# Four chained layers in one kernel: seams between stages joined, a mixing product cut into pieces and run among attention scores, and a top-4 choice made with an eight-largest instruction

## What is computed

```python
for l in range(4):
    xn = layernorm(x)
    x = x + attn[l](xn) * silu(ffn[l](xn))
```

```python
# layer 0 attn: gated linear recurrence; its last step adds a bias
out = h_m @ W_out + b_out
# layer 0 ffn: shared expert + 8 experts, two chosen by the router's logits = x @ router_w
# layer 1 attn: selective scan; starts with W_in, W_skip, a convolution over 4 taps
# layer 1 ffn: dense 1024-wide; layer 2 attn: 16 heads of 16, one key head
# layer 2 ffn: 16 experts, four chosen, at most 128 tokens an expert, and a shared expert
scores = softmax(x @ gate_w.T); topk_w, topk_i = top_k(scores, 4)
y = scatter_add(expert outputs); return y + shared
# layer 3 attn: 16 heads, keys and values from a latent of 64 numbers a token
probs = softmax(q @ kv.T * scale); out = (probs @ kv) @ W_o
# layer 3 ffn: weights in four bits
inter = gelu(x @ Wg.T) * (x @ Wu.T); out = inter @ Wd.T
```

## Time and profile before

| what | us |
|---|---|
| median of 3 runs | 1033.92 (1033.4 to 1038.56) |
| profiled execution, its own time | 1034.3 |
| its span | 1032.5 |
| PE busy | 948.9 (92%) |
| DVE busy | 696.2 (67%) |
| ACT busy | 480.4 (47%) |
| POOL busy | 279.5 (27%) |

### The profile page before, as it was taken

One profiled execution on the slowest core, in us unless ns is written; L12 is line 12 of the kernel. 1 busy time (PEld: TensorE's weight loads), 2 busy tenths in 40 slices (PEclk: granted clock), 3 DMA queues, 4 the chain that ended last, 5 costly groups with the idle time before them and its releaser, 6 DMA issues. The chain is left out here.

```text
span 1032.5 us, 13682 instructions
## 1 busy us (share of the span) xinstructions
PE 948.9 (92%) x4708; PEld 568.6 (55%) x4708; DVE 696.2 (67%) x1092; ACT 480.4 (47%) x1008; POOL 279.5 (27%) x244
## 2 busy tenths in 40 slices
PE   4999998999999999999999999887889859999997
PEld 2555564365665666655555555565466535555554
DVE  2789867369998999759545555674775735566653
ACT  3542224799887887322135555535664611111112
POOL 0000000008887888420014233102643520000000
PEclk9899999999999999999999999999999989999999
DMA  4112205040000000028045443221000001111101
GB/s 130 43 66 77 71 11 178 1 119 26 22 22 21 22 21 1 2 85 250 1 131 112 91 111 84 56 62 41 2 1 2 1 1 31 61 31 30 30 1 41
DMA packets 58303, 53.89 MB, mean 52 GB/s; under 512 B 14216, under 2 KB 53224, under 8 KB 58240
## 3 DMA queue, kind: packets, MB, share of 16 engines
q1 hardware_dynamic: 52704, 47.05, 15.2%
q0 software_dynamic: 3072, 4.20, 2.5%
q10 hardware_dynamic: 2464, 1.84, 0.6%
HBM read 44.45 MB, written 5.47 MB: 48 GB/s over the span
## 5 line engine op out<-in xcount | busy, mean ns | idle before, releaser
L1085 POOL TENSOR_TENSOR seen<-state,c_row 128x512 f32<-128x512 f32 x128 | 160.7, 1278 | 101.4 <-DVE state L1105 74.2
L1105 DVE TENSOR_TENSOR_SCAN state<-decay,banks 128x512 f32<-128x512 f32 x128 | 155.3, 1217 | 14.8 <-issue 7.3
L2526 PE MATMUL banks<-xnT,weight 128*128 128x512 f32 x256 | 115.0, 592 | 1.1 <-PEq L2221 1.1
L1043 ACT ACTIVATE weighed_x<-dx_tok,b_tok 128x512 f32<-128x512 f32 x124 | 87.6, 709 | 25.7 <-PE banks L1215 24.4
L2237 POOL TENSOR_TENSOR prob<-prob,inverse 128x512 f32<-128x512 f32 x64 | 65.3, 1041 | 116.4 <-DVE inverse L2324 116.4
L1053 ACT ACTIVATE decay<-delta_pairs,A 128x510 f32<-128x510 f32 x128 | 90.5, 707 | 6.2 <-DVE state L1105 6.2
L1215 PEld LDWEIGHTS banks<-ident,weighed_x 128*128 128x128 f32 x512 | 58.6, 140 | 59.2 <-ACT weighed_x L1043 33.3
L2558 ACT ACTIVATE gelu<-banks 128x512 f32<-128x512 f32 x32 | 19.1, 597 | 138.1 <-PE banks L2526 138.1
L1215 PE MATMUL banks<-ident,weighed_x 128*128 128x128 f32 x512 | 80.1, 279 | 2.3 <-DVE state L1105 2.3
L2526 PEld LDWEIGHTS banks<-xnT,weight 128*128 128x128 f32 x256 | 48.6, 190 | 49.4 <-issue 47.9
L1229 PE MATMUL banks<-seen,fold 128*64 128x512 f32 x256 | 69.7, 617 | 0.0
(11 more groups left out here) (382 smaller groups left out, 1717.0 us busy)
## 6 DMA issues: line engine op xcount, KB each, us to landing
prob_row<-probs_dram SPq DMA_DIRECT2D x8, 512.0 KB, 3.7
c_row<-c_dram SPq DMA_DIRECT2D x32, 128.0 KB, 2.8
slot_wide_w<-in_L_ffn_w_gate SPq DMA_DIRECT2D x16, 176.0 KB, 2.4
slot_wide_w<-in_L_ffn_w_up SPq DMA_DIRECT2D x16, 176.0 KB, 2.5
slot_down_w<-in_L_ffn_w_down SPq DMA_DIRECT2D x16, 176.0 KB
gate_up_w<-in_L_ffn_gate_up_w SPq DMA_DIRECT2D x8, 256.0 KB, 2.7
delta_pairs<-conv_in SPq DMA_DIRECT2D x8, 256.0 KB
w_WqT<-in_L_attn_W_q SPq DMA_DIRECT2D x1, 2048.0 KB, 10.5
```

The costliest lines, as they stand in the source:

```text
L1043: nc.scalar.activation(weighed[:, v % 2, tile, :, j, :], dx_tok[:, 4 * p + tile, :].rearrange("p (g e) -> p g e", g=groups), ACT.Identity, ...
L1085: nc.gpsimd.tensor_tensor(seen[:, u % ring, :], state[:, u % ring, :], c_row[:, v % 4, :], ALU.mult).then_inc(seen_ready, 1)
L1105: nc.vector.tensor_tensor_scan(state[:, u % ring, :], decay[:, u % ring, :, :].rearrange("p b t -> p (b t)"), banks[:, 4 + u % 2, :], 0.0, ...
L2526: last = nc.tensor.matmul(banks[:, 4 + 2 * half + j, :], weight[:, s, j, k, tile * P:(tile + 1) * P], xnT[:, k, cols[half]], start=(k == 0 ...
```

## The change

It touches eight places.

1. `earlier` moves to the end of `loads0`: the first block waits for `ident` alone, the norm stage for the rest.
2. The router's 16 matmuls of layer 0 are issued four after each of the four W_in groups.
3. Layer 0's bias: x gets `gated * b_out` before the mixed product is there, for tiles 0 to 3 on DVE, for tiles 4 to 7 on POOL. The gate's multiply then reads PSUM itself, and L687 is gone. The 7 fillers stay.
4. Layer 1's loads are issued as `norm_w`, W_in, W_skip, five small ones, five others, with a semaphore for each part; PE waits for W_in and W_skip first, DVE and ACT for the small ones, PE for the others before W_d1.
5. In `route_stage` `rank_mask` gives way to `top_mask`; a fourth job goes before the wait for `chosen`, and the five fillers are gone.
6. The table product goes ahead of the shared expert's down product, the three fillers go. SP no longer waits for the store of y, nor for the other weights before it issues layer 3's loads; POOL waits for the store before its first scatter.
7. `mix(0)` and `mix(1)` are cut into pieces of 4, 3, 3, 3, 3 matmuls, one after each of the units 2 to 6 of the next sequence; `mix(2)` goes behind the last scores, its copy goes from DVE to ACT.
8. `FourBitJobs`: the first two of the 32 four-bit jobs (`widen`, gelu, multiply) go into the attention stage, job 0 between `mix(2)` and `weigh(3)` and job 1 between `weigh(3)` and `mix(3)`, in banks that scores have left.

```diff
+def top_mask(nc, steps, mask, values, scratch, experts, top):
+    shape = [P, NT, experts]
+    best, above, equal, rank, count, same_row = scratch
+    for t in range(NT):
+        steps.add(nc.vector.max(best[:, t, :], values[:, t, :]))
+    steps.join()
+    last = best[:, :, top - 1:top].broadcast_to(shape)
+    steps.add(nc.vector.tensor_tensor(above, values, last, ALU.is_gt))
+    steps.do(nc.vector.tensor_tensor(equal, values, last, ALU.is_equal))
+    steps.add(nc.vector.tensor_tensor_scan(rank.rearrange("p t e -> p (t e)"), same_row, equal.rearrange("p t e -> p (t e)"),
+                                           0.0, ALU.mult, ALU.add))
+    steps.do(nc.vector.tensor_reduce(count, above, AX.X, ALU.add))
+    steps.do(nc.vector.tensor_tensor(rank, rank, count.unsqueeze(2).broadcast_to(shape), ALU.add))
+    steps.do(nc.vector.scalar_tensor_tensor(equal, rank, float(top), equal, ALU.is_le, ALU.mult))
+    steps.do(nc.vector.tensor_tensor(mask, above, equal, ALU.add))
...
+def add_bias(nc, waits, engine, b, x_tok, scratch, gated, bias, gate_ready, done):
+    pair = slice(2 * b, 2 * b + 2)
+    waits.wait_ge(gate_ready, b + 1)
+    engine.tensor_tensor(scratch[:, pair, :], gated[:, pair, :], bias[:, :].unsqueeze(1).broadcast_to([P, 2, D]), ALU.mult
+                         ).then_inc(done, 1)
+    waits.wait_ge(done, 2 * (b % 2) + 1)
+    engine.tensor_tensor(x_tok[:, pair, :], x_tok[:, pair, :], scratch[:, pair, :], ALU.add).then_inc(done, 1)
...
-                sp.wait_ge(*rest_weights)
                 for dst, src in next_loads:
                     sp.dma_start(dst, src).then_inc(next_loaded, DMA)
+                sp.wait_ge(stored, 2 * DMA)
                 sp.wait_ge(y_ready, NT // 2)
-                sp.dma_start(by_token(y_dram[0:N, :]), y_shared[:, :, :]).then_inc(stored, DMA)
-                sp.wait_ge(stored, 3 * DMA)
+                sp.dma_start(by_token(y_dram[0:N, :]), y_shared[:, :, :]).then_inc(y_stored, DMA)
...
+    mix_parts = {2: (0, 4), 3: (4, 7), 4: (7, 10), 5: (10, 13), 6: (13, 16)}
...
-                    if batch_after(u, 4) is not None:
-                        mix(batch_after(u, 4))
+                    b, unit = place(u)
+                    if 1 <= b < BATCH - 1 and unit in mix_parts:
+                        mix(b - 1, *mix_parts[unit])
+                mix(BATCH - 2)
+                pe.wait_ge(exp_ready, 2 * (pairs - 1))
+                jobs.widen(pe, 0, 0, 0)
                 weigh(BATCH - 1)
                 pe.wait_ge(exp_ready, 2 * pairs)
+                jobs.widen(pe, 0, 1, 2)
                 mix(BATCH - 1)
```

266 lines of the change are left out of this document (155 added, 111 removed).

## The result

The changed kernel takes 1010.93 us, the median of 4 runs (1009.35 to 1012.4); the kernel before, beside it, 1036.24 (1033.4 to 1040.56). The ratio is 0.975, 95% interval 0.971 to 0.980. The direction was right. The time lies 8.9 us above the forecast of 1002.0 and 1.9 above the upper end of the range, 1009.

A forecast was written before the change was run, and what follows sets the result against it. PE was taken as the bound, busy 92% of the span, with waits, fillers and 1.2 GHz time to be had. Eight terms summed to 32.65 us off 1034.3; with 0.35 for late arrivals, 1002.0 us, range 998 to 1009.

The forecast's parts named there:

- the term for the route's end: Route stage's end: table first, no fillers, no wait for the store of y; 2.7 us less, bounds 0 and 2.7.
- the term for the router: Layer 0's gates: quarters between wide groups keep 2.4 GHz; 2.1 us less, as DVE is late next; bounds 0 and 2.8.
- rival A: Down product starts at 1.2 GHz and the quarters do not hold the clock: 1004 to 1007 us; chance 0.25.
- First block: Kernel start: without the wait for `earlier`, PE starts near 8.1 instead of 12.27; 4.1 us less, bounds 0 and 4.6.
- layer 1's loads: Layer 1's start: W_in and W_skip issued earlier, so ACT ends the wait; 1.25 us less, bounds 0 and 1.3.
- bias: Layer 0's end: DVE work leaves the tail but PE's fillers still bind; 0.1 us less, bounds -0.5 and 0.3.
- PE's wait at 49.29 hangs on this DVE chain: Layer 0: DVE's ranking and coefficients limit the router's gain to 2.1 us, not the 2.8 saved on PE.
- Choice of experts: Layer 2's route stage: MAX8 and narrow steps remove fillers and wait before `chosen`; 6.1 us less, DVE having 3 us of cover.
- Rival C: Layer 2's expert weights land late behind the store, at most its 4.9 us come back: 1003 to 1007 us; chance 0.1.
- Mix in pieces: Layer 3's attention: pieces no longer hold scores back; 2.95 us less for each of two sequences, 5.9 together.
- the end of the attention: Layer 3: earlier last score and early four-bit jobs fill waits before first `lower`; 10.5 us less, bounds 8 and 10.8.
- Rival B: Layer 3's attention: PE meets as many waits as before, so the 5.9 us stay: 1008 us; chance 0.12.

The follow-up runs named there:

- fill_5: Changed kernel with 5 instead of 7 fillers at layer 0's end; 1010.05 us, ratio 0.972.
- seams_alone: Kernel before with points 1 to 4 of the change alone; 1033.34 us, ratio 0.995.
- latent_busy: Changed kernel with small fillers in the waits at the start of layer 3's attention; 1006.49 us, and 1005.25 us the second time.
- table_woven: Changed kernel with the narrow table matmuls spread over the first four tiles of the shared expert's down product; 1014.31 us, ratio 0.975.
- changed_again: The changed kernel, unaltered, run a second time; 1008.87 us, ratio 0.970.
- no_fill_scores: Changed kernel without the three fillers behind the first two score jobs of layer 2's attention; 1010.58 us, ratio 0.972.

## Why the prediction was right and where it was wrong

The direction and six of the eight terms were right. What failed is the clock: the term for the route's end took the removal of fillers and the narrow row ahead of real work to cost nothing, the term for the router did the same for a longer wait, and rival A priced all of it at 5 us at the most, where 9.4 came. The base of the sum, one execution at the quick end of its kernel's times, hid another 4.3.

*First block, layer 1's loads, bias.* Right: 4.4 for 4.1, and 1.5 for 1.35 together. ACT's function table now ends the block (at 7.56), and the fillers bound layer 0's seam, as fill_5 shows.

*Router in quarters.* The mechanism was right and so was its size: the first gate took 3.70 us in all seventeen traces with quarters, and 5.4 to 6.5 in the three with the row; where the first expert job kept the clock too, 2.1 to 2.2 us were gained. But the step "PE's wait at 49.29 hangs on this DVE chain" was read only for its length. The first expert job started 2.0 us sooner after PE's first matmul, as summed. But the wait ahead of it became 2.26 us instead of 1.66, and behind it the job ran at the low clock 12 times of 14: 1.6 to 1.7 us of the 2.1 went there.

*Choice of experts.* Right. `chosen` was ready at 461.3, long before PE came for it at 465.76; 4.5 us of cover for the 3 forecast.

*Route's end.* The failed term: 2.7 forecast, and 0.2 lost in its place, 18.50 us instead of 18.34 from the last shared job to the next stage. The sentence that failed is "by the rows the removal costs nothing". One trace in which a narrow row did not lower the clock was taken for a rule; in seams_alone the same code had the low clock right behind the same row. Fifteen traces have the new order. From the table's start to the next stage four of them took 15.45 us, at full clock, two 17.1, and nine 18.2 to 18.6, the changed kernel's three among these. So the waits and the work were summed rightly, and the clock was not. No run puts the fillers back in this place, so how much their removal did and how much the order did stays open. Then 2.8 more went behind it, which no rival had: score products and fillers at 1.2 GHz ahead of the gathered tokens, which had landed 3 us before PE took them. Rival C did not come: no wait for a weight of the experts appeared.

*Mix in pieces and the end of the attention.* Right in size, 6.1 for 5.9 and 10.7 for 10.5; of the 6.1 only 5.1 are the pieces' own. Rival B fell.

*Rival A* is what happened, and it was priced too low: 2 to 5 us for two places. There were four, 9.4 us together: after the wait in layer 0 (1.7), in the down product (2.7), at the next stage's start (2.8) and at the start of layer 3's attention (2.2). The last is in untouched code. My text had it that stretches at 1.2 GHz "that the change does not touch may fall elsewhere", and used it for the low side of the range alone.

The Trainium skill ("TensorE: Matmul & The Clock Gate", Part 1, What's actually happening) says two things that bear on this. That activity releases the throttle: latent_busy agrees, with 1.00 instead of 0.73 when the waits were filled; table_woven does not, where the profile shows PE busy without a gap and at 1.2 GHz for 17 us. And that one kernel measures differently from run to run in how much runs at the low clock: the two traces of latent_busy's program agree, with a down product of 13.47 and of 10.64 us.

*The base.* The sum was made against one execution of 1034.3 us, with a mean clock of 0.987. The 52 runs of the kernel before average 1038.6. The runs that I had, 1033.4 to 1038.56, showed a spread of 5 us, and I set the profiled execution against their median without asking which of them it resembled. By arithmetic the 8.9 us are made up like this: 4.3 because the base was at the low end of its kernel's times; 3.2 because the change gains 1038.6 - 1009.5 = 29.1 us in the mean, not the 32.3 of the sum with its allowance; and 1.4 because the four runs of the result lay above the changed kernel's own mean. In the means of all runs, then, the change fell short of its sum by a tenth; these means are uncertain by about 1.3 us (an estimate from the spread of the runs), so the shortfall is clear of that.

What stays open is what decides, in one execution, whether the same row at the same place lowers the clock. The runs show that it varies between executions of one program, and that at the one place where waits were filled the low clock became rarer, and no more.

## What to carry to other kernels

A gain from removing fillers, waits or wide work around narrow work is to be summed at full clock and then charged for each place behind it where PE waits or runs narrow rows, also in code that the edit leaves alone: here 1.7 to 2.8 us each. Try small fillers in waits that exist anyway (0.3 to 2.7 us gained at the one place where it was tried), and don't count on spreading narrow work to do the same: it held the clock in layer 0 and not in layer 2. And before summing against one profiled execution, compare its mean granted clock with those of the other runs.

## What the runs showed of the hardware

- One program's time followed its mean granted clock at 6.3 us for each 0.01 (the changed kernel; 8.1 for the kernel before), and its executions ranged over 8 us (1004.4 to 1012.4), over 6.7 us (1004.4 to 1011.1) in the six runs of changed_again alone.
- PE stayed at 1.2 GHz for 17 us while it was busy without a gap, in a mix of 6-column and 256-column matmuls and then in 256-column ones alone (table_woven).
- The same indirect gather, beside the same store and loads, landed 5.1 or 5.2 us after its issue in the three traces of the changed kernel, 6.1 us after it in latent_busy, which is the same program up to that point, and 6.6 in no_fill_scores; no run shows why.
- The choice of the four largest of 16 scores for 1024 tokens took 2.9 us with eight MAX8 (0.71 together) and seven steps over 128 elements or fewer (changed kernel), and 11.7 us with steps over 2048 elements (kernel before).
